# All sixteen diagonal blocks of a head group masked by GpSimd in the exponents instead of six of them by products on TensorE

## What is computed

```python
qkv = (x @ w_qkv).reshape(B, S, 3, H, D)
q = _unit_norm(q); k = _unit_norm(k)            # then rope on every second head
logits = jnp.einsum('bshd,bthd->bhst', q, k) * q_gain[None, :, None, None]
causal = jnp.tril(jnp.ones((S, S), dtype=bool))
logits = jnp.where(causal[None, None], logits, jnp.finfo(logits.dtype).min)
attn = jax.nn.softmax(logits, axis=-1)
y = jnp.einsum('bhst,bthd->bshd', attn, v).reshape(B, S, Dm)
```

## Time and profile before

| | us |
|---|---|
| three runs | 1038.08, 1038.64, 1041.03 (median 1038.64) |
| profiled execution | 1034.4 |
| its span | 1032.7 |
| attention ends about | 528 |

### The profile page before, as it was taken

One profiled execution on the slowest core, in us unless ns is written; L12 is line 12 of the kernel. 1 busy time (PEld: TensorE's weight loads), 2 busy tenths in 40 slices (PEclk: granted clock), 3 DMA queues, 4 the chain that ended last, 5 costly groups with the idle time before them and its releaser, 6 DMA issues.

```text
span 1032.7 us, 17543 instructions
## 1 busy us (share of the span) xinstructions
PE 999.6 (97%) x5951; PEld 724.4 (70%) x5951; DVE 651.0 (63%) x1138; ACT 547.3 (53%) x906; POOL 376.6 (36%) x312
## 2 busy tenths in 40 slices
PE   6899999999999999999999999999999999999996
PEld 7564566646666455664367778889999999998885
DVE  5699584896849968398679666444334333324776
ACT  4778776687767867668846632223333333321213
POOL 0332132321323312131534107563475666424431
PEclk9999999999999999999999999999999999999998
DMA  6447333473342723418146206593455553414433
GB/s 205 129 117 213 95 103 97 108 215 92 102 132 84 224 73 102 123 52 252 44 129 188 78 31 229 191 289 120 156 166 166 166 168 116 145 53 126 135 110 123
DMA packets 115821, 140.60 MB, mean 136 GB/s; under 512 B 10272, under 2 KB 74016, under 8 KB 115744
## 3 DMA queue, kind: packets, MB, share of 16 engines
q1 hardware_dynamic: 83552, 102.56, 33.4%
q10 hardware_dynamic: 27072, 20.20, 6.2%
q0 software_dynamic: 5120, 16.78, 5.0%
HBM read 83.93 MB, written 55.57 MB: 135 GB/s over the span
## 4 chain that ended last, share of the span: by engine, by line
PE 77%; DVE 10%; ACT 6%; DMA 2%; POOL 2%; issue 2%; SPq 0%; DVEq 0%; ACTq 0%
PE scores L634 15%; PE scores L1529 10%; PE bank L1482 10%; PE scores L694 8%; PE bank L1579 8%; PE bank L622 8%; PE bank L739 5%; PE scores L542 4%; ACT probs L1683 4%; DVE key_sum L1808 4%; PE bank L1576 3%; DVE x L1164 1%; PE scores L602 1%; POOL wqkv_l L1886 1%; PE bank L1588 1%
## 5 line engine op out<-in xcount | busy, mean ns | idle before, releaser
L1683 ACT ACTIVATE probs<-scores,shift_now 128x1024 f32<-128x1024 f32 (+3 forms) x296 | 273.5, 978 | 74.1 <-PE scores L1529 48.8
L1808 DVE TENSOR_TENSOR key_sum<-key_sum,probs 128x2048 f32<-128x2048 f32 (+1 forms) x96 | 205.3, 2138 | 50.7 <-PE bank L1579 19.1
L1529 PEld LDWEIGHTS scores<-q_stack,k_stack 96*128 96x128 f32 x624 | 99.2, 188 | 121.6 <-ACT probs L1683 66.1
L1529 PE MATMUL scores<-q_stack,k_stack 96*128 96x512 f32 (+3 forms) x624 | 177.1, 396 | 6.6 <-ACT probs L1683 2.8
L1579 PE MATMUL bank<-probs,v_sb 128*32 128x512 f32 (+3 forms) x1184 | 135.8, 533 | 0.0
L634 PE MATMUL scores<-ffn_w,xt_h 128*128 (+1 forms) x608 | 125.1, 328 | 0.0
L1044 DVE TENSOR_TENSOR ht_l<-scores,ht_h 128x256 fp32r<-128x256 f32 x39 | 16.6, 425 | 142.2 <-ACT ht_h L827 142.2
L634 PEld LDWEIGHTS scores<-ffn_w,xt_h 128*128 128x128 f32 x608 | 101.0, 189 | 3.5
L1263 POOL TENSOR_TENSOR ffn_w<-raw,ones 128x1408 fp32r<-128x1408 f32 (+4 forms) x32 | 64.1, 2014 | 97.6 <-PE bank L622 78.7
L1558 POOL TENSOR_SCALAR_AFFINE_SELECT probs<-probs 128x512 f32<-128x512 f32 x40 | 44.3, 1115 | 136.4 <-ACT probs L1683 136.4
L694 PE MATMUL scores<-x1T_h,ffn_w 128*128 128x512 f32 x352 | 89.5, 391 | 0.0
(11 more groups left out here) (254 smaller groups left out, 1760.2 us busy)
## 6 DMA issues: line engine op xcount, KB each, us to landing
k_stack<-turn_scratch SPq DMA_DIRECT2D x48, 256.0 KB, 4.3
q_stack<-turn_scratch SPq DMA_DIRECT2D x45, 256.0 KB, 3.9
x_sorted<-zeros SPq DMA_DIRECT2D x39, 256.0 KB, 3.5
y_sorted<-y_tile ACTq DMA_DIRECT2D x39, 256.0 KB, 2.9
x_tile<-x_sorted ACTq DMA_DIRECT2D x148, 64.0 KB, 2.0
turn_scratch<-turned_h SPq DMA_DIRECT2D x31, 256.0 KB, 2.1
turn_scratch<-turned_l SPq DMA_DIRECT2D x31, 256.0 KB, 2.3
raw<-w_gate SPq DMA_DIRECT2D x8, 704.0 KB, 5.2
```

The costliest lines, as they stand in the source:

```text
L1529: mm = nc.tensor.matmul(scores[:, p, hh, lo:CH], k_stack[0:3 * HD, h, j * P:(j + 1) * P], q_stack[0:3 * HD, i % 2, h, lo:CH], start=True, ...
L1683: nc.scalar.activation(exponents(g, slot)[:, 2 * p:2 * p + 2, lo:CH], scores[:, p, :, lo:CH], ACT.Exp, bias=shift_now[:, p:p + 1]).then_in ...
L1808: nc.vector.tensor_tensor(key_sum[:, :, lo:CH], key_sum[:, :, lo:CH], probs[:, slot % 4, :, lo:CH], ALU.add).then_inc(sum_dve, 1)
```

## The change

The set of slots masked by a product becomes empty. So lines 1532 and following make no instruction (the score products stop their accumulation themselves), `is_selected` holds for all sixteen diagonal slots, and GpSimd's program gets an `affine_select` at slots 7, 20, 21, 22, 38 and 39 of each group, ahead of what stands there for the same slot and behind what stands at earlier slots.

```diff
-MASK_BY_PRODUCT = {7, 20, 21, 22, 38, 39}
+MASK_BY_PRODUCT = set()
```

## The result

| | before, us | after, us |
|---|---|---|
| five runs each, on one chip | 1039.06 (1038.08 to 1041.03) | 1084.34 (1082.83 to 1093.52) |
| profiled execution / its span | 1034.4 / 1032.7 | 1093.5 / 1091.8 |
| first product behind attention (line 542) | 527.64 | 579.77 |

After over before is 1.0462, 95% interval 1.0436 to 1.0489: the change costs about 45 us. Where the two differ, both are given.

The account below looks back on a forecast made before the run. TensorE, busy 97%, was taken as the bound. Terms 10.0 + 17.5 + 0.7 + 4.55 + 6.0 + 3.2 = 41.95 us on the profiled 1034.4, plus 4.2 to the median, gave 1080.6, said as 1080; range 1067 to 1093.

Parts of the forecast that it names:

- The order of GpSimd's program sets the price: Slots 7 and 38: new selects queue behind GpSimd's rotations of slots 6 and 37; waits sum to 10.0 and 17.5 us.
- The waits at slot 7 and at the ends: TensorE's values later by 2.9 us at slot 7 (1.45 in group 1), 5.8 to 5.9 at ends of groups 0 to 2.
- rival 4: All slots: GpSimd hides every select and TensorE gets 6.7 us of products back, 1032 us; chance 0.02.
- rival 3: Slots 7, 38, 39: no waits behind rotations, for instance because these get done much earlier; about 1041 us; chance 0.05.
- Group 1's slot 7: Slot 7 of group 1: TensorE is already late, so its wait for the mask is only 1.45 us.
- Slots 20 to 22: Selects contend with VectorE's additions: 1.3 us a group, between 0.3 and 2.3; 3.9 us for three groups.
- In group 3 (1.35 us given with its end): Group 3: VectorE's last addition, awaited before the sums at 488.02, ends about 0.65 us later; 0.7 us more at slots 38, 39.
- The clock: Low clock behind TensorE's waits: three ends at 2.0 us each, two slot 7 waits at 1.6 each; 9.2 us.
- The waits are the other part: The forecast's sum without its clock terms: 41.95 less 9.2 us.
- Rival 2: All six long waits lower the clock (14.4 us), slots 20 to 22 cost 2.3 a group: about 1089 us; chance 0.14.
- the half behind attention is unchanged in length: Behind attention: the MoE half was to keep its length in the profile of after.

Follow-up runs that it names:

- e4: The changed kernel with GpSimd's rotation of slot 6 put behind the select of slot 7, and that of slot 37 behind those of 38 and 39: 1044.05 us.
- e1: Kernel before with only slot 7 of the change masked by GpSimd, the other five slots keeping mask products: 1046.47 us, ratio 1.0126.
- e2: Kernel before with only slots 38 and 39 of the change masked by GpSimd: 1056.75 us, ratio 1.0228.
- e3: Kernel before with only slots 20, 21 and 22 of the change masked by GpSimd: 1038.94 us, ratio 1.0049.
- e8: Kernel before with only slot 20 of the change masked by GpSimd: one run, 1036.83 us against 1036.65.
- e5: As e4, but slots 20 to 22 keep their mask products: 1041.14 us, ratio 1.0019.
- e6: As e2, plus 26 unread TensorE products ahead of the values of slot 38 in groups 0 to 2: 1053.11 us, ratio 1.0151.
- e9: As e1, plus ten unread TensorE products ahead of the values of slot 7 in each group: 1045.38 us, ratio 1.0063.
- e10: As e3, but key sums of slots 20 to 22 made by TensorE products with ones instead of VectorE's additions: one run, 1042.36 us against 1036.65.

## Why the prediction was right, and where it wasn't

1080.6 us were worked out and 1084.34 measured, within the range of 1067 to 1093. The three parts alone measured 12.8, 23.1 and 5.3 us where the prediction's terms give 13.2, 24.2 (17.5 + 6.0 + 0.7) and 4.55.

- **The order of GpSimd's program sets the price.** Held. The waits at slot 7 and at the ends are ended by the select with the rotation directly ahead of it, and 2.70 and 6.2 us long. (2.9 and 5.8 to 5.9 were given as the delay of the values; at the ends the wait also holds the twice 0.28 us that TensorE comes earlier. At slot 7 of group 2 the delay, counted from the start of line 1775, is 2.77.) e4 keeps every select and loses both waits with the order alone. That TensorE would get its products back (rival 4) needed GpSimd to be free when asked, and a share of 36% doesn't say that; rival 3's condition, a rotation out of the way, is what e4 built by hand.
- **Group 1's slot 7** was wrong: 1.45 us in the prediction, 2.70 measured in both profiles of after. Step that failed: the earlier trace rows took TensorE's delay by the DMA of `k_stack` from one execution, as if it belonged to the kernel. That wait comes and goes: e1, e2, e3 and e8 have it (0.8 to 1.3 us), and e4, e5, e6, e9, e10 and both profiles of after don't have it in that place. Where it is there, the wait for the mask is shorter, 1.86 us in e1. It doesn't go by the delay at the end of group 0: e2 has that delay and the wait, e9 and e10 have neither. Why it comes and goes stays open. The end of group 2 is alike: the profile of before had waited 2.16 us with a low clock behind it, the other kernels in which that end is unchanged (e1, e3, e8, e9, e10) didn't, and so it grew by 4.5 us only where the other two ends grew by 7.4 to 9.2.
- **Slots 20 to 22** were right where the clock stayed up: 1.3 us given, 1.45 and 1.60 measured in groups 2 and 1, and 1.42 in group 0 of e3. The selects of 1.85 us show the mechanism, and e10 confirms it by its absence. The rule of the Trainium skill cited in the prediction (page "SBUF — State Buffer", section "SBUF: two separate sides") agrees in both directions: the select waits for the addition, and an operation of VectorE that reads two inputs (line 1747, which takes `inv_norm` twice) waits for the select, 0.67 us instead of 0.19 in e4. Two things failed. In group 0 the clock fell behind waits of about 1 us each, and the stage took 3.8 us. In group 3 (1.35 us given with its end) the price was put on a wait that isn't in the row: TensorE doesn't wait before the sums at 488.02. It waits for the selects themselves, 0.77, 1.09 and 0.38 us in e3, whose last stage grew by 1.9; with e2's 1.2 that makes 3.1 without any low clock, and after has 5.2 and 3.7.
- **The clock** was the mis-sized term. Given: five stretches, 2.0 and 1.6 us each, 9.2 in all. The accounts above have 21.5 us in one profile and 13.6 in the other, whose execution (1085.2 us) is near the median. Found: nine stretches in one and seven in the other; 1.6 to 3.2 us for each end, so the 2.0 given was near; 1.4 to 2.8 for each slot 7 that has one, four of them and two, where two at 1.6 were given; 2.4 for slots 20 to 22 of group 0, and up to 2.1 in group 3, where nothing was given. The waits are the other part: idle time grew by 37.3 and 38.0 us, less the 6.7 of saved products 30.6 and 31.3, where 32.75 were given. They are that near partly by luck, as DMA waits of before that aren't in after took 2.8 and 1.5 us off. Rival 2 had this mechanism (the clock falls more often and costs more, slots 20 to 22 are dearer), and its 1089 is about as far from the median as the forecast's 1080. So the total doesn't choose between them; the profiles speak for a clock term between the two forecasts' or above both.
- **The single parts** agree with their terms better than the stages do. In e1 12.8 us stand beside 13.2, but its slot 7 stages grew by 16.9, and 3.7 us were given back at the end of group 2, which is luck.
- **That the half behind attention is unchanged in length** can't be said to better than its own spread, 503.7 to 512.0 us in twelve profiles; short and long ones share no edit. It may also be why the profiled execution of before, with one of the short ones, lies 4 us under its median.

What stays open: why the clock falls behind waits of 1.09 and 0.84 us in slots 21 and 22 of group 0 in both profiles of after, and not behind the same waits in e3 and e4. Those two have no long wait at slot 7, so it may matter; but in groups 1 and 2 of after such a wait stands ahead too, and the clock doesn't fall behind slots 20 to 22, whose second wait is 0.38 us there. No run separates the two. Nor is it known why the DMA waits of the earlier trace rows come and go, or what stops ScalarE behind attention.

## What to carry to other kernels

Before work goes to an engine that looks idle, read where in its in-order program the new instruction stands and when what is ahead of it can start: here a select of 0.64 us cost 2.7 or 6.2 us, and moving two rotations took three quarters of the loss away. Price a wait on TensorE at its length plus the low clock behind it, and give that as a spread: here nothing to 2.8 us behind waits of 2.70 us, and 1.5 to 3.2 us behind waits of 6.2. Filling the wait with products that nobody reads separates the two. And a wait for a DMA that one profile shows may be missing in the next execution, so look for it in several before a sum is built on it.

## What the runs showed of the hardware that wasn't expected

The granted clock fell to 0.50 behind two waits of about 1 us each (group 0 at 109 us, 6 us long), and stayed at 1.00 behind the same two in e3 and e4. Of the four waits at slot 7 (1.8 to 2.7 us), all were followed by the low level in one execution of after and two in the next, and a low stretch behind equal waits cost 1.4 to 1.5 us or 2.8, so a forecast of the clock is a spread and not a number. It fell behind waits for a DMA as well, of 1.66 and 2.25 us in e5. A select of 128x512 holds up VectorE's small operations, with one input and with two: of those of 128x32, 0.18 us became 0.62 (line 1761, one input) and 0.19 became 0.67 (line 1747, two), which made the chain to the next group 0.4 to 0.5 us longer for each select beside it.
